# A graph layer on one core: three wide VectorE operands move to a PSUM bank, and the edge products rotate through three banks

## The reference, cut to what matters

```
xn = layernorm(x)
x  = x + gat(xn) + mix(xn)          # mix: linear attention, 8 heads, then a norm, two dense layers, a norm
x  = x + ffn(layernorm(x))          # 8 experts of three dense layers, summed with router weights

gat: h = xn @ W_src (4 heads x 64);  e = leaky(a_src[src] + a_dst[dst]);  m = segment_max(e, dst)
     p = exp(e - m[dst]);  out[n] = sum over edges into n of p * h[src]  /  sum of p
     then bias, layernorm, prelu
```

## Time and profile before

| | us |
|---|---|
| median of 3 runs | 4558.61 |
| lowest and highest | 4550.4, 4563.28 |
| the profiled execution, its own time | 4551.85 |
| its span in the profile | 4549.9 |
| TensorE, VectorE, ScalarE, GpSimd busy (share of the span) | 4134 (91%), 3823 (84%), 2277 (50%), 1888 (41%) |
| gathers L857: number, busy in all | 1664, 1824.0 |
| messages L976: number, busy in all | 832, 562.6 |
| adds L991: number, busy, idle before them | 1664, 792.4, 208.2 |

### The profile page before, as it was taken

How to read it: one execution, slowest core, us unless ns; L and a number is a source line. 1 busy time by engine, 2 the same in 40 slices (tenths; PEclk the granted TensorE clock), 3 DMA queues, 4 the chain that set the end, 5 groups by cost and what they waited for, 6 DMA issues and landing times. The chain is left out here.

```text
span 4549.9 us, 85744 instructions
## 1 busy us (share of the span) xinstructions
PE 4134.0 (91%) x23003; PEld 3316.4 (73%) x23004; DVE 3823.0 (84%) x9879; ACT 2277.0 (50%) x4346; POOL 1888.1 (41%) x1702
## 2 busy tenths in 40 slices
PE   8984898889988988998898884999999999999999
PEld 7873666666666666666666653888888888888888
DVE  8875889888988899898989886787887878878786
ACT  5552344344334334443434333666666666666666
POOL 2117777777777777777777730000000000000000
PEclk9996999999999999999999987999999999999999
DMA  5545777777777777777777753000000000000000
GB/s 193 170 142 149 206 205 227 213 209 208 226 211 208 210 223 208 208 221 218 210 206 220 211 164 93 23 21 28 14 28 20 22 28 14 28 24 19 28 14 19
DMA packets 440077, 601.76 MB, mean 132 GB/s; under 512 B 41560, under 2 KB 366704, under 8 KB 439920
## 3 DMA queue, kind: packets, MB, share of 16 engines
q1 hardware_dynamic: 360048, 378.47, 25.8%
q0 software_dynamic: 79872, 221.62, 19.7%
HBM read 312.68 MB, written 287.25 MB: 132 GB/s over the span
## 5 line engine op out<-in xcount | busy, mean ns | idle before, releaser
L857 POOL DMA_INDIRECT acc<-h_tab,strips x1664 | 1824.0, 1096 | 538.4 <-issue 518.0
L1362 PE MATMUL ps<-acc 128*128 128x260 f32 x3328 | 1011.1, 432 | 24.1 <-DVE acc L991 16.1
L991 DVE SCALAR_TENSOR_TENSOR acc<-acc,strips,ps 128x260 f32<-128x260 f32 x1664 | 792.4, 476 | 208.2 <-PE ps L1362 176.8
L1362 PEld LDWEIGHTS ps<-acc 128*128 128x128 f32 x3328 | 621.0, 207 | 112.7 <-DVE acc L991 22.4
L976 DVE TENSOR_TENSOR acc<-acc 128x512 f32<-128x512 f32 x832 | 562.6, 681 | 0.0
L1896 ACT ACTIVATE exp<-ps,bn 128x512 f32<-128x512 f32 (+1 forms) x400 | 310.2, 775 | 452.7 <-PE ps L1963 449.0
L1961 PE MATMUL ps<-w_hi,b_hi 128*128 128x256 f32 x1568 | 444.8, 284 | 1.2 <-DVE exp L1799 1.2
L1963 PE MATMUL ps<-w_hi,b_lo 128*128 128x256 f32 x1568 | 443.5, 283 | 0.0
L1962 PE MATMUL ps<-w_lo,b_hi 128*128 128x256 f32 x1568 | 443.5, 283 | 0.0
L1179 ACT ACTIVATE strips<-ps 128x512 bf16<-128x512 bf16 x416 | 247.6, 595 | 276.9 <-PE ps L1338 259.0
L1807 DVE TENSOR_TENSOR a_lo<-exp,a_hi 128x512 fp32r<-128x512 f32 (+1 forms) x400 | 258.7, 679 | 147.3 <-ACT a_hi L1898 132.2
(11 more groups left out here) (271 smaller groups left out, 8325.5 us busy)
## 6 DMA issues: line engine op xcount, KB each, us to landing
side_tab<-acc SPq DMA_DIRECT2D x416, 520.0 KB
acc<-h_tab,strips POOLq DMA_INDIRECT x1664
acc<-xnt_tab SPq DMA_DIRECT2D x50, 512.0 KB
h_tab<-proj SPq DMA_DIRECT2D x25, 520.0 KB, 6.7
exp<-side_tab SPq DMA_DIRECT2D x100, 130.0 KB, 2.3
proj<-in_x SPq DMA_DIRECT2D x25, 512.0 KB, 5.3
base_tab<-proj SPq DMA_DIRECT2D x25, 512.0 KB, 3.2
xnt_tab<-proj SPq DMA_DIRECT2D x25, 512.0 KB, 6.0
```

Source lines behind the costliest of these rows:

```text
L857: pool.indirect_dma_start(G[s][:, b * GU + u], None, h_tab, bass.IndirectOffsetOnAxis(REC[s][:, b * GU + u, 0:1], 0)).then_inc(g_in[s], 16)
L991: nc.vector.scalar_tensor_tensor(A[:, (b % 2) * GU + u], A[:, (k - 1) % (2 * GU) if k else 2 * GU], smt[s][:, k:k + 1], ps[u][:, 0:MW], AL ...
L1362: nc.tensor.matmul(ps[u][:, 0:MW], S32[b % 2][:, u], G[s][:, b * GU + u], start=True, stop=True).then_inc(g_mm.sem, 1)
```

## The change

The products use banks 0 to 2 in rotation, by k mod 3 over all steps, and step k waits for the add of three steps before. The steps of a turn number 32, so step 0 waits for step 30 of the last turn, step 1 for 31 and step 2 for 29. The fourth bank, ps[3], now holds three things that ScalarE writes: a copy of the row numbers (IOTA_PS), the row g2 in two halves (G2_PS), both once at the stage's beginning, and the factors exp(df) (PF), once a turn, by a second exponential in front of the old one. Three VectorE operations read them there: onehot (in the loop; the first three comparisons before the loop still read SBUF), message, and o_scale. o_scale and o_finish are each cut into two halves, placed before add 2 and behind add 3 of their batches.

```diff
--- before.py
+++ after.py
@@ -297,6 +297,10 @@
         bstats, bmv = rm.take(2, CH, 6), rm.take(2, CH, 2)
         brs, btv, btt, nb = rm.take(2, CH), rm.take(2, CH), rm.take(2, CH), rm.take(2, CH)
         T4 = ps[4][:, 0:D].bitcast(bf16)
+        BANKS = 3
+        IOTA_PS, PF = ps[BANKS][:, 0:P], ps[BANKS][:, P:2 * P]
+        G2_PS = [ps[BANKS][:, (2 + j) * P:(3 + j) * P] for j in range(2)]
+        ps_set = sem("ps_set")
         LB = 5
         MIX = ps[5]
 
@@ -308,7 +312,7 @@
         u_mm, u_ev, o_mm, o_cp = stage("u_mm", 4), stage("u_ev", 4), stage("o_mm", 2), stage("o_cp", 2)
         ln_st = [stage(f"{v}_st", 2) for v in ("m", "o")]
         ln_ag, ln_rs, ln_nb = stage("ln_ag"), stage("ln_rs", RSQ), stage("ln_nb")
-        o_norm, o_g, o_base = stage("o_norm"), stage("o_g"), stage("o_base")
+        o_norm, o_g, o_base = stage("o_norm"), stage("o_g", 2), stage("o_base", 2)
 
         win_in, win_f, pick_set, rec_mm, rec_ev = (stage("win_in", 16), stage("win_f"), stage("pick_set"), stage("rec_mm"),
                                                    stage("rec_ev"))
@@ -382,14 +386,14 @@
             nc.vector.scalar_tensor_tensor(pick, t, w_col[0:GS, 0:1], t0.broadcast_to([GS, GS]), ALU.subtract,
                                            ALU.is_equal).then_inc(pick_set.sem, 1)
 
-        def onehot(dve, q, sq, b):
+        def onehot(dve, q, sq, b, numbered):
 
             dr_set.wait(dve, q)
             s_ev.wait(dve, q - 2, b + 1)
             t_mm.wait(dve, q - 2, b + 1)
             d = dr[sq][:, b * GU:(b + 1) * GU].unsqueeze(2).broadcast_to([P, GU, P])
             nc.vector.tensor_tensor(SB[sq][b].rearrange("p (u n) -> p u n", u=GU),
-                                    iota_row[:, :].unsqueeze(1).broadcast_to([P, GU, P]), d, ALU.is_equal
+                                    numbered.unsqueeze(1).broadcast_to([P, GU, P]), d, ALU.is_equal
                                     ).then_inc(s_set.sem, 1)
 
         def numbers(act, r):
@@ -612,8 +616,8 @@
 
             dve.wait_ge(old_set, 2)
             relative(dve, 0, 0)
-            onehot(dve, 0, 0, 0)
-            onehot(dve, 0, 0, 1)
+            onehot(dve, 0, 0, 0, iota_row[:, :])
+            onehot(dve, 0, 0, 1, iota_row[:, :])
             for k in range(KC):
                 compare(nseg, k)
             cmp_mm.wait(dve, nseg)
@@ -875,6 +879,7 @@
                 dve.wait_ge(ad_cut, 4)
                 nc.vector.tensor_copy(adb[:, :, 2], ad_rest).then_inc(ad_cut, 1)
                 dve.wait_ge(ed_set, 1)
+                dve.wait_ge(ps_set, 3)
 
                 def gaps(q):
 
@@ -972,9 +977,9 @@
 
                     p_exp.wait(dve, g)
                     lo = b * GU + 2 * i
-                    m = G[s][:, lo:lo + 2].rearrange("p t (h c) -> p t h c", c=HB)
-                    nc.vector.tensor_tensor(m[:, :, :, 0:HB - 1], m[:, :, :, 0:HB - 1],
-                                            m[:, :, :, HB - 1:HB].broadcast_to([P, 2, HEADS, HB - 1]), ALU.mult
+                    m = G[s][:, lo:lo + 2].rearrange("p t (h c) -> p t h c", c=HB)[:, :, :, 0:HB - 1]
+                    f = PF.rearrange("p (h t) -> p t h", h=HEADS)[:, lo:lo + 2]
+                    nc.vector.tensor_tensor(m, m, f.unsqueeze(3).broadcast_to([P, 2, HEADS, HB - 1]), ALU.mult
                                             ).then_inc(msg_set.sem, 1)
 
                 def add(g, s, b, u):
@@ -989,7 +994,7 @@
                     if u == 0:
                         used(dve, side_out[b % 2], 16, g * (GQ // 2) + b // 2)
                     nc.vector.scalar_tensor_tensor(A[:, (b % 2) * GU + u], A[:, (k - 1) % (2 * GU) if k else 2 * GU],
-                                                   smt[s][:, k:k + 1], ps[u][:, 0:MW], ALU.mult, ALU.add
+                                                   smt[s][:, k:k + 1], ps[k % BANKS][:, 0:MW], ALU.mult, ALU.add
                                                    ).then_inc(acc_add.sem, 1)
 
                 def q_elu(c, m):
@@ -1038,15 +1043,16 @@
                     nc.vector.scalar_tensor_tensor(nb[:, both], bmv[:, both, :, 0], -1.0, brs[:, both], ALU.mult, ALU.mult
                                                    ).then_inc(ln_nb.sem, 1)
 
-                def o_scale(c):
+                def o_scale(c, h):
                     o_norm.wait(dve, c)
-                    nc.vector.tensor_tensor(TM, TM, row(R_G2).unsqueeze(1).broadcast_to([P, CH, D]),
-                                            ALU.mult).then_inc(o_g.sem, 1)
-
-                def o_finish(c):
+                    v = TM[:, :, h * P:(h + 1) * P]
+                    nc.vector.tensor_tensor(v, v, G2_PS[h].unsqueeze(1).broadcast_to([P, CH, P]), ALU.mult).then_inc(o_g.sem, 1)
+
+                def o_finish(c, h):
                     o_g.wait(dve, c)
                     bx_in.wait(dve, c)
-                    nc.vector.tensor_tensor(BX, BX, TM, ALU.add).then_inc(o_base.sem, 1)
+                    t = slice(2 * h, 2 * h + 2)
+                    nc.vector.tensor_tensor(BX[:, t], BX[:, t], TM[:, t], ALU.add).then_inc(o_base.sem, 1)
 
                 def mix_between(n, i):
 
@@ -1062,9 +1068,9 @@
                     if i == 10:
                         deviations(n)
                     if prev and i == 14:
-                        o_scale(n - 1)
+                        o_scale(n - 1, 0)
                     if prev and i == 15:
-                        o_finish(n - 1)
+                        o_finish(n - 1, 0)
 
                 def mix_after(n, i):
 
@@ -1073,6 +1079,10 @@
                         denominators(n)
                     if cur and i in (4, 5):
                         quotients(n, i - 4)
+                    if prev and i == 14:
+                        o_scale(n - 1, 1)
+                    if prev and i == 15:
+                        o_finish(n - 1, 1)
 
                 def turn(g, s, n, q, sq, nq, r):
                     here, ahead = g is not None, q is not None
@@ -1114,13 +1124,13 @@
                             mix_between(n, s * GQ + b)
                             add(g, s, b, 2)
                         if ahead and b < GQ - 2:
-                            onehot(dve, q, sq, b + 2)
+                            onehot(dve, q, sq, b + 2, IOTA_PS)
                         if q2 is not None:
                             if b == GQ - 2:
                                 relative(dve, q2, 1 - sq)
-                                onehot(dve, q2, 1 - sq, 0)
+                                onehot(dve, q2, 1 - sq, 0, IOTA_PS)
                             if b == GQ - 1:
-                                onehot(dve, q2, 1 - sq, 1)
+                                onehot(dve, q2, 1 - sq, 1, IOTA_PS)
                         if here:
                             add(g, s, b, 3)
                             mix_after(n, s * GQ + b)
@@ -1146,6 +1156,10 @@
 
             @block.scalar
             def _(act):
+                nc.scalar.activation(IOTA_PS, iota_row[:, :], ACT.Copy).then_inc(ps_set, 1)
+                for j in range(2):
+                    nc.scalar.activation(G2_PS[j], rows[:, R_G2 + j * P:R_G2 + (j + 1) * P], ACT.Copy).then_inc(ps_set, 1)
+
                 def same_steps(q, sq):
 
                     acc_add.wait(act, q - 2)
@@ -1205,6 +1219,8 @@
 
                 def exponent(q, sq):
                     p_df.wait(act, q)
+                    msg_set.wait(act, q - 1)
+                    nc.scalar.activation(PF, df, ACT.Exp)
                     nc.scalar.activation(heads_of(sq), df.rearrange("p (h t) -> p h t", h=HEADS), ACT.Exp).then_inc(p_exp.sem, 1)
 
                 def shrink_exp(q):
@@ -1355,11 +1371,12 @@
                     if i == 0:
                         s_ev.wait(pe, g, b + 1)
                     for u in (2 * i, 2 * i + 1):
-                        if b:
-                            acc_add.wait(pe, g, (b - 1) * GU + u + 1)
+                        k = b * GU + u
+                        if k >= BANKS:
+                            acc_add.wait(pe, g, k - BANKS + 1)
                         else:
-                            acc_add.wait(pe, g - 1, (GQ - 1) * GU + u + 1)
-                        nc.tensor.matmul(ps[u][:, 0:MW], S32[b % 2][:, u], G[s][:, b * GU + u], start=True, stop=True
+                            acc_add.wait(pe, g - 1, 1 + max(j for j in range(GS) if j % BANKS == k))
+                        nc.tensor.matmul(ps[k % BANKS][:, 0:MW], S32[b % 2][:, u], G[s][:, b * GU + u], start=True, stop=True
                                          ).then_inc(g_mm.sem, 1)
 
                 def spread(q):
```

## The result

The kernel after takes 4594.99 us (4593.34 to 4597.56, 4 runs), the one before in the same study 4559.73 (4550.4 to 4563.28, 4 runs): ratio 1.0081, 95% interval 1.0064 to 1.0098. In a later study it was 4594.32 against 4559.04, 1.0078 (1.0064 to 1.0092). It is slower by 35 us. The forecast of record was 4619, with 4595 to 4645 as its own band, so the measured time lies at the band's lower edge.

A forecast was written before the change was run, and what follows sets the result against it. VectorE and TensorE in turns were taken to pace the edge stage's usual pair. 65 + 4 - 9 = +60 on the profiled 4551.85 gave 4612, against the median 4619; own band 4595 to 4645, range 4550 to 4662.

The forecast's parts named there:

- Part 1: One SBUF operand less in comparison, message and o_scale: no operation shorter, gathers about 1.0 us; -9 us, between -3 and -31.
- the bound of 61 us from L991: Upper price of the PSUM operands on VectorE: 0.05 us x 24 x 51, if all lay on the path.
- the -9: Gain from shorter gathers: some 5 us at the stage's beginning, 4 us off the first turns of some five slow pairs.
- Part 2: Three banks for the products: later products delay TensorE's dense block; 65 us over 25 full pairs, bounds 45 and 83.
- Product 13's 0.15: Second turn: product 13 awaits add 10 and costs what sticks out of a comparison, 0 to 0.45 us, taken as 0.15.
- The cover of 0.2 us behind product 31: Product 31 awaits add 28, ScalarE's L1213 ends later but before L968 needs it: nothing, 0.3 us a pair if misjudged.
- Part 3: Halves of o_scale and o_finish at the pair's end: 4 us (0 to 8); second exponential, its wait and start copies: nothing.
- the one for TensorE's clock: Low-clock stretches in second turns, 2.4 us each: share of 0.3 to 0.4 kept; none would give -22 us, all +41.
- GpSimd as the pace: Edge stage: gathers set the pace, 89.6 us against 88.9 a pair; 4521 in the profile, 4528 by the median; chance 0.12.
- The hidden wait: Bank wait at turn starts: TensorE catches up before VectorE asks; about 4554 us; chance 0.10.
- Slower still by the clock: New pauses at each turn's beginning make TensorE's clock fall more often: 4660 us; chance 0.18.
- The 79 us of the rule for PSUM sources: VectorE's PSUM reads: 58 cycles fixed for SBUF, 120 for PSUM, 0.065 us x 24 x 51; the prediction doubted it.

The follow-up runs named there:

- 31 gathers: Kernel before with the last gather of each group left out from group 2 on, those steps using old rows: 4544.14 us, ratio 0.9965.
- the repeated run: The kernel after, unchanged, run again in a later study on a chip like the first: 4594.32 us.
- the new order: At a turn's start TensorE does product 2, dense block, register loads, then product 3; on the kernel after, 4564.58 us on a chip like the first.
- the first, failed reordering: Kernel after with the dense block between products 2 and 3 (30 and 31) in batches 0 and 7, loads still behind product 3: 4609.72 us.

## Why the prediction was right, and where its size was off

**What bounds the stage.** Right. VectorE and TensorE in turns pace the usual pair: fewer gathers leave it at 88.9, gathers of 0.97 and of 1.07 us give 91.8 and 91.9, one wait of TensorE moves it by 2.8.

**Part 1.** L982 takes 676 ns and L395 681: no operation got longer, as taken from L1011, and the bound of 61 us from L991 fell away. The gathers went to 0.97 us (forecast about 1.0); 0.03 of the 0.13 came with the slower pace of the rotation alone (1.065). L1208 has no DMA wait left but one of 5.1 us at the start, where L1194 had 10.6. Of the -9, the 5 at the beginning are 3.9 in the first four turns. The other 4, from slow first turns, did not come. Before, five of the 21 first turns took 41.6 to 41.8 us and not 40.9; after, nine take 42.9 to 43.3 and not 42.4, although the gathers are shorter. One of these:

```profile
1695.60:1738.90 43.30, 40.01 (x216) 29.39 (x215) 38.48 (x96) 16.07 (x37) 29.45 (x32) 0.92 0.81 240
```

Its clock is 0.92, where the first turn of 42.4 us above has 1.00. The five slow first turns before have 0.92 as well. So the 0.7 of such a turn goes with the clock, and a shorter gather did not take it off, as the prediction had it; that the slow first turns are gone with 31 gathers leaves a part of the gathers in it open.

**Part 2.** Forecast +1.46 in the first turn and +1.0 in the second. Measured in the pair shown: 1.5 at add 12 (13.69 after add 0 before, 15.19 now) and 1.0 at add 8 (9.79 and 10.80). Product 13's 0.15 was 0.28, found at add 20 (27.61 and 28.90). The cover of 0.2 us behind product 31 held for VectorE: L973 at the pair's end follows the operation before it by 0.03 us, as L968 did by 0.04. For TensorE it did not: product 31's wait makes products 0 to 2 of the next turn 1.5 us late, and the prediction followed its late block no further than L968. It came out all the same because both waits end in the same delay and do not add up; that is luck. The prediction's sign, TensorE idle before product 3 at every turn's start, came only half true: 24 first turns show it, 0.23 us in the one above, and hardly a second turn. That product 3's wait alone is enough was shown by the kernel with it alone (usual pair 91.6), and that the late block is what costs by the order that takes the wait out of its way (89.9).

**Part 3.** The halves: the second turn is longer by 1.38 in the median (48.05 and 49.43), of which the two steps above explain 1.29; the 0.1 left answers to the 0.14 forecast, but it wasn't isolated: with three banks alone, without the halves, the second turn has 49.38 already.

**The sum.** 2.61 and 0.16 a pair were forecast, 2.77; the usual pair grew by 2.8 to 2.9. Yet the profile grew by 45.7 and not by 60. The term that was mis-sized most is the one for TensorE's clock: "I keep that share; none would give -22 us". Before, 7 of 21 second turns had a long stretch at the lower clock, at 2.4 us each; after, 1, and in the repeated run none. 6 x 2.4 = 14 us. The -22 was the right end of that range. That 14 is just the difference between 60 and 45.7 is chance, because smaller misses cancel. By stretches the 45.7 is made up so: turns 5 to 46 grew by 47.9 (21 usual pairs by 2.85 are 60, the six slow second turns -15, the slow first turns +3), the last six turns by 5.9, the time before the first add by 0.8; the first four turns lost 3.9 and the ffn stage 5.0 (below). The medians differ by 35 only, because the profiled execution of before lies 7.9 under the median of its study and that of after 2.6 above its own: the forecast moved its sum up to the median and had to assume that the next profile would lie there too.

**The rivals.** GpSimd as the pace: refuted for the usual pair; one gather in 32 was worth 14 us at most in the four-bank kernel, and shorter gathers some 8 us in the first four turns with three banks (190.0 against 182.3). The hidden wait: refuted; add 4 waits 1.15 us. Slower still by the clock: the clock went the other way, 0.94 to 0.97. The 79 us of the rule for PSUM sources that the prediction quotes did not come: 676 ns with one operand in PSUM against 681.

**Open.** Why the long stretches at the lower clock vanish in the kernels whose product 3 waits, and return when it does not. The counts, each from one execution, are 0, 0, 1 and 0 slow second turns with the rotation in the old order, 4, 11 and 11 with the new order, 7 before and 4 with 31 gathers: fewer where the pairs are longer. But 10 in the first, failed reordering and 3 with product 3's wait alone do not fit that. Open too is what product 31's wait costs by itself, and what the new order does with four banks on a chip like the first. No kernel that does all of the work beat the one before; the nearest is the kernel after with block and loads ahead, 0.2% above it.

## What to carry to other kernels

A buffer less in a rotation costs little at most steps and much at a few: look for the steps whose release lies behind other work of the releasing engine, here 3, 13, 19 and 31 of 32, and see what stands behind each in the waiting engine's in-order queue. The length of a wait is not its price: here the longest (product 13) took the place of an older one, and product 3's showed only 0.23 us, because TensorE came late already. If such a step can't be freed, put the long independent block ahead of it, together with whatever register loads that block was hiding; here that gave back 30 of 35 us.

When TensorE runs near its limit, count the stretches at the lower clock before pricing a change: where pairs got shorter there were more of them, 2.4 us each, and a usual pair of 89.8 went with a longer program than one of 89.9. Their number can differ between executions (1 and 0 in the two profiles of the kernel after), so it wants more than one profile.

## What the hardware showed beside

- Moving one of VectorE's two wide inputs from SBUF to PSUM left its own time alone (681 to 676 ns). With the rotation held the same, three such operands shortened GpSimd's indirect gathers from 1065 to 967 ns; the message's operand alone makes 88 ns of these.
- The ffn stage, whose code is the same in all kernels, takes 1816.3 us before and 1811.3 after. From the last add to the end it was 1815.5 to 1817.6 in the five kernels without operands in PSUM on chips like the first, and 1809.6 to 1811.3 in the six profiles with the row numbers and the norm's scale there, factors or not. Its cause is not known; it is 4 of the 16 us that the operands and halves gave.
- One chip ran the kernel before in 5014.69 us and not 4559, by pauses of up to 7 us common to three engines. The same kernel had a ratio of 1.042 there and 1.0018 on the first kind of chip. Kernels to be compared must run on one chip, with the kernel that they change beside them.
